# Graph network, node projection: x and its weights split into a high and a low reduced-precision part

## The chip, the cores and the metric

One core of one Trainium2 chip runs the whole program in one launch. The metric is the device time of a launch in microseconds (us), the median of several runs. Beside the timed runs one execution was recorded by the hardware profiler; all rows shown come from it.

## The reference

50,000 nodes with 256 features, 50,000 edges sorted by destination. A graph attention layer, a layer norm, a message-passing layer with a three-layer network, and a second layer norm. The part that matters here is the projection at the start:

```python
loops = jnp.arange(n)                       # a self loop for every node
x_proj = (x @ lin_W.T).reshape(n, 4, 64)    # 50000 x 256 by 256 x 256
s_src = jnp.einsum('nhd,hd->nh', x_proj, att_src)
s_dst = jnp.einsum('nhd,hd->nh', x_proj, att_dst)
att = s_src[src] + s_dst[dst]               # + edge term, leaky relu, softmax over dst
...
out = segment_sum(x_proj[src] * alpha, dst) + bias
x = layernorm(x + out)
x = layernorm(x + message_passing(x, edge_attr_128, src, dst, ...))
```

All arrays are float32.

## The kernel before, in words

The program is a row of blocks with a barrier between them: setup of weights, projection, ranking of the edges by their other end, gathering and attention, the first layer norm with the first products of the second network (`n_` names), the edge network (`u_` names), and the last layer norm. The change touches the setup and the projection block.

**Setup.** The weights are loaded by SyncE and ScalarE queues. VectorE splits the weights of the second network (w0r, w1r, w2r, wgr) into a high part of the type fp32r (a shorter float32 that TensorE takes as one product) and a low part, the rest. TensorE transposes lin_W and multiplies it by the attention vectors; VectorE copies the result from PSUM (the accumulator memory, 8 banks) to `wst`, 128 x 2 x 264: 256 columns of lin_W.T and 8 of attention terms, for two halves of the 256 input features.

**Projection.** The nodes are padded to 98 groups of G = 4 tiles of 128 rows. `groups` writes out four groups, then a loop of two groups a turn, then two more; all engines run the same walk over the groups, and semaphores hold them together. For group g:

- SyncE loads `xin` (128 x 4 x 256), two buffers.
- TensorE (`body`, L382 on) first counts the edges' destination digits: four matmuls of 128 x 392 in f16 from one-hot tiles `ohlo` and `ohhi` into bank 6 (L385), all accumulated over the whole block. It waits for `h_oh`, which VectorE raises once per group, after the fourth pair of one-hot tiles. Then it transposes xin of group g+1 into banks 0 and 1 (`transposes`, L377, eight of 128 x 128). Then come the projections of group g (L394): for each of the four tiles j two float32 matmuls (k = 0, 1) of `xT` with `wst` into bank 2+j, after VectorE has emptied that bank (`pr_d`).
- ScalarE (`both`, L461) copies banks 0 and 1 of group g+1 to `xT`.
- VectorE (`body` from L430) works on two groups at once: for each j it makes the one-hot pair j of group g+1 (`one_hots`, L327 and L328), then waits for the projection of tile j of group g and adds the bias to it (L438, bank to `xps`).
- GpSimd stores `xps` to the DRAM tensor XP.

Each engine takes its instructions in the order in which they are written (TensorE's weight loads may run ahead beside the matmul before them).

Of the kernel before, what the change touches and what calls it, by code (L numbers as in the profile page):

```python
# [21 lines left out]
P = 128  # L22
G = 4
HEADS = 4
# [32 lines left out]
def gnn_kernel(nc, x, src, dst, e128, e32, lin_W, att_src, att_dst, lin_edge_W, att_edge, bias,  # L57
# [90 lines left out]
    with top:  # L148
# [18 lines left out]
        upto = alloc(top, "upto", [P, P])  # L167
        after = alloc(top, "after", [P, P])
        iota = alloc(top, "iota", [P, max(NT, P)], f16)
        wst = alloc(top, "wst", [P, 2, XW])  # L170
        wedge = alloc(top, "wedge", [P, 4 * HEADS])
        biasx = alloc(top, "biasx", [P, XW])

# [14 lines left out]
        with ph:  # L188
# [6 lines left out]
            le4 = alloc(ph, "le4", [P, 2, 4, KE])  # L195
            ab = alloc(ph, "ab", [P, 2, 3 * HEADS])
            ioi = alloc(ph, "ioi", [P, max(NT, P)], i32)
            s_zero, s_load, s_const = sem("w_zero"), sem("w_load"), sem("w_const")
            s_attl, s_mm, s_ev = sem("w_att"), sem("w_mm"), sem("w_ev")
            with nc.Block() as block:  # L200
                @block.gpsimd
# [18 lines left out]
                @block.sync  # L220
                def _(sp):
                    sp.wait_ge(s_zero, 1)
                    with nc.allow_non_contiguous_dma(reason="small weight vectors"):
                        for k, a in enumerate((att_src, att_dst, att_edge)):
                            for h in range(HEADS):
                                r = (h % 2) * HD
                                sp.dma_start(ab[r:r + HD, h // 2, k * HEADS + h:k * HEADS + h + 1],
                                             a[h, :].rearrange("(d a) -> d a", a=1)).then_inc(s_attl, 16)
                        for r, k, a, n in [(0, k, a, n) for k, (a, n) in enumerate(M0[:3])] + \
                                          [(r, 3, A0, R0) for r in STACK]:  # L230
                            sp.dma_start(b0s[r:r + n, k:k + 1], b0[a:a + n].rearrange("(d a) -> d a", a=1))\
                                .then_inc(s_load, 16)
                        for k, (a, n) in enumerate(M1):
                            sp.dma_start(b1s[0:n, k:k + 1], b1[a:a + n].rearrange("(d a) -> d a", a=1))\
                                .then_inc(s_load, 16)
                    sp.wait_ge(s_load, 16 * 9)

                @block.scalar
                def _(act):
                    act.dma_start(lw[:], lin_W.rearrange("(c p) i -> p c i", p=P)).then_inc(s_attl, 16)  # L240
                    for r in range(4):
                        act.dma_start(le4[:, :, r, :], lin_edge_W.rearrange("(c p) k -> p c k", p=P))\
                            .then_inc(s_attl, 16)
                    act.dma_start(biasx[:, 0:D], bias.partition_broadcast(P)).then_inc(s_attl, 16)
                    act.dma_start(w0s[:], W0.rearrange("(c p) m -> p c m", p=P)).then_inc(s_attl, 16)
                    for k, (a, n) in enumerate(M0[:3]):
                        act.dma_start(w1s[0:n, k, :], W1[a:a + n, :]).then_inc(s_attl, 16)
                    act.wait_ge(s_zero, 1)
                    for r in STACK:
                        act.dma_start(w1ts[r:r + R0, :], W1[A0:F0, :]).then_inc(s_attl, 16)  # L250
                    for k, (a, n) in enumerate(M1):
                        act.dma_start(w2s[0:n, k, :], W2[a:a + n, :]).then_inc(s_attl, 16)
                    a, n = M1[-1]
                    act.dma_start(w2s[n:n + 1, 2, :], b2.rearrange("(a d) -> a d", a=1)).then_inc(s_attl, 16)
                    act.dma_start(wgs[:], Wg).then_inc(s_attl, 16)
                    act.wait_ge(s_attl, 16 * (3 * HEADS + 18))

                @block.vector
                def _(dve):
# [4 lines left out]
                    c.did(nc.vector.memset(biasx[:, D:XW], 0.0))  # L264
                    c.did(nc.vector.memset(KI[:, :, NT:NT + G], 0))
                    c.did(nc.vector.memset(wedge[:], 0.0))
                    dve.wait_ge(s_attl, 16 * (3 * HEADS + 18))
                    parts = [(w0r, w0s, P, slice(0, 4)), (wgr, wgs, P, None)]
                    parts += [(w1r, w1s, n, k) for k, (a, n) in enumerate(M0[:3])]
                    parts += [(w2r, w2s, n + (k == 2), k) for k, (a, n) in enumerate(M1)]  # L270
# [11 lines left out]
                            c.did(nc.vector.tensor_copy(w1t[:], w1ts[:]))  # L282
                        c.wait()
                    dve.wait_ge(s_mm, 1)
                    for k in range(2):
                        c.did(nc.vector.tensor_copy(wst[:, k, 0:D], B[k][:, 0:D]))
                    dve.wait_ge(s_mm, 2)
                    for k in range(2):
                        c.did(nc.vector.tensor_copy(wst[:, k, D:XW], B[2 + k][:, 0:8]))
                    c.wait()  # L290
                    for r in range(4):
                        c.did(nc.vector.tensor_copy(wedge[r * KE:(r + 1) * KE, r * HEADS:(r + 1) * HEADS],
# [2 lines left out]
                @block.tensor  # L295
                def _(pe):
                    pe.wait_ge(s_const, 8)
                    pe.wait_ge(s_attl, 16 * (3 * HEADS + 18))
                    for k in range(2):
                        for c in range(2):  # L300
                            t = nc.tensor.transpose(B[k][:, c * P:(c + 1) * P], lw[:, c, k * P:(k + 1) * P], ident[:])
                    t.then_inc(s_mm, 1)
                    for k in range(2):
                        for c in range(2):
                            nc.tensor.matmul(B[2 + k][:, 0:8], lw[:, c, k * P:(k + 1) * P], ab[:, c, 0:8],
                                             start=(c == 0), stop=(c == 1))
                    for c in range(2):
                        t = nc.tensor.matmul(B[4][:, 0:HEADS], le4[:, c, :, :].rearrange("p r k -> p (r k)"),
                                             ab[:, c, 8:12], start=(c == 0), stop=(c == 1))
                    t.then_inc(s_mm, 1)  # L310
# [4 lines left out]
        with srt:  # L315
# [17 lines left out]
            ph = ExitStack()  # L333
            with ph:
                xin = [alloc(ph, f"xin{s}", [P, G, D]) for s in range(2)]
                xT = [alloc(ph, f"xT{s}", [P, 2, G * P]) for s in range(2)]
                xps = [alloc(ph, f"xps{s}", [P, G, XW]) for s in range(2)]
                kr = [alloc(ph, f"key_rows{q}", [P, NC, P], i32) for q in range(2)]
                krf = [alloc(ph, f"key_rowsf{q}", [P, NC, P]) for q in range(2)]
# [2 lines left out]
                tot = [alloc(ph, f"tot{q}", [P, NT]) for q in range(2)]  # L342
                cum = alloc(ph, "cum", [P, NT])
                x_loaded, xp_stored = sems("p_x_loaded"), sems("p_xp_stored")
                xt_psum, xt_a = sem("p_xt_psum"), sem("p_xt_act")
                pr_psum, pr_d = sem("p_pr_psum"), sem("p_pr_dve")
                h_pad, h_loaded, h_rows, h_psum = sem("h_pad"), sem("h_loaded"), sem("h_rows"), sem("h_psum")
                h_chain, h_oh, h_acc, h_hist, h_sums = sem("h_chain"), sem("h_oh"), sem("h_acc"), sem("h_hist"), sem("h_sums")
# [4 lines left out]
                with nc.Block() as block:  # L353
# [17 lines left out]
                    def _(pe):  # L371
                        def transposes(g, s, i, last):
                            pe.wait_ge(x_loaded[s], 16 * (i + 1) + 16 * last)
                            for k in range(2):
                                need(pe, xt_a, 2 * (g - 1) + k + 1)
                                for j in range(G):
                                    t = nc.tensor.transpose(XB[k][:, j * P:(j + 1) * P],  # L377
                                                            xin[s][:, j, k * P:(k + 1) * P], ident[:])
                                t.then_inc(xt_psum, 1)

                        def body(g, s, i, last):
# [5 lines left out]
                            t.then_inc(h_acc, 1)  # L387
                            if not late(g, 1):
                                transposes(g + 1, 1 - s, i if s == 0 else i + 1, late(g, 2))
                            pe.wait_ge(xt_a, 2 * (g + 1))  # L390
                            for j in range(G):
                                need(pe, pr_d, 4 * (g - 1) + j + 1)
                                for k in range(2):
                                    t = nc.tensor.matmul(OB[j][:, 0:XW], xT[s][:, k, j * P:(j + 1) * P], wst[:, k, :],  # L394
                                                         start=(k == 0), stop=(k == 1))
                                t.then_inc(pr_psum, 1)
                        pe.wait_ge(h_rows, 2)
                        for q in range(2):
# [10 lines left out]
                    def _(dve):  # L409
# [13 lines left out]
                        for q in range(2):  # L423
                            c.did(nc.vector.tensor_copy(LO[q][:], ki[q][:]))
                            c.did(nc.vector.tensor_copy(HI[q][:], ki[2 + q][:]))
                        c.wait()
                        for j in range(G):
                            one_hots(0, 0, j, h_oh, (0,))

                        def body(g, s, i, last):  # L430
                            need(dve, xp_stored[s], 16 * i)
                            if not late(g, 1):
                                need(dve, h_acc, g)
                            for j in range(G):
                                if not late(g, 1):
                                    one_hots(g + 1, 1 - s, j, h_oh, (0,))
                                dve.wait_ge(pr_psum, 4 * g + j + 1)
                                nc.vector.tensor_tensor(xps[s][:, j, :], OB[j][:, 0:XW], biasx[:], ALU.add).then_inc(pr_d, 1)  # L438
                        groups(dve, body)
                        dve.wait_ge(h_acc, GROUPS)  # L440
                        nc.vector.tensor_copy(hist[:], HB[:, 0:NT]).then_inc(h_hist, 1)
# [14 lines left out]
                    def _(act):  # L456
                        def both(g, s):
                            need(act, pr_psum, 4 * (g - 1))
                            for k in range(2):
                                act.wait_ge(xt_psum, 2 * g + k + 1)  # L460
                                nc.scalar.copy(xT[s][:, k, :], XB[k][:]).then_inc(xt_a, 1)  # L461

                        def body(g, s, i, last):
                            if not late(g, 1):
# [1319 lines left out]
```

## Time and profile before

| | us |
|---|---|
| median of 3 runs | 5411.32 |
| lowest and highest run | 5406.67, 5420.93 |
| profiled execution | 5421.3 |
| its span | 5419.7 |

| engine | busy us | share of the span |
|---|---|---|
| TensorE matmul (PE) | 4311.3 | 80% |
| TensorE weight load (PEld) | 3429.3 | 63% |
| VectorE (DVE) | 3819.4 | 70% |
| ScalarE (ACT) | 2759.3 | 51% |
| GpSimd (POOL) | 3366.1 | 62% |

The busy shares are means over blocks with different limits. The projection block lies at about 28 to 565 us of the span. In the rows, PEclk and "granted clock" are the mean TensorE clock that the throttle granted, as a share of the full 2.4 GHz; 0.50 is the lower level, 1.2 GHz. A float32 matmul of L394 stands in the trace as two records, every other matmul used here as one. "Idle before" is the time the engine stood still just ahead of an instruction, with what released it. Names are given as out<-in.

### The profile page before, as it was taken

The page shows a single profiled execution, that of the slowest core. Times are in us where ns is not written, and L with a number is a line of the kernel's source. Part 1 is how long each engine was busy: PE and PEld are TensorE (multiplying, and loading weights), DVE is VectorE, ACT ScalarE, POOL GpSimd, SP SyncE. Part 2 cuts the span into 40 slices and gives each one's busy share as a digit, 9 for nine tenths or more (in the row PEclk, how much of TensorE's full clock was granted, in tenths as well). Part 3 has the DMA queues.
Part 4 walks back from the last instruction along what each step waited for, and adds up shares of the span by engine and source line. Part 5 has one row for each costly group of instructions (what it writes and reads, how often), then busy time and mean ns, then how long its engine had stood idle before and what let it go on. Part 6 is the DMA issues. An engine that isn't in the chain of part 4 may idle for free. (4 is left out here: it accounts for less than half of the span.)

```text
span 5419.7 us, 98490 instructions
## 1 busy us (share of the span) xinstructions
PE 4311.3 (80%) x23300; PEld 3429.3 (63%) x23300; DVE 3819.4 (70%) x12680; ACT 2759.3 (51%) x6177; POOL 3366.1 (62%) x3119
## 2 busy tenths in 40 slices
PE   7999777777756676599999997999999999999400
PEld 5777433333334444599999996877877777777300
DVE  5666777777756666798989884766666666666564
ACT  1212233333323333366666665777777777777475
POOL 1111677777777776455555545777777777777432
PEclk9999887888878888799999998999999999999755
DMA  5666100000027666699999995666666666666496
GB/s 159 200 202 200 37 9 9 9 9 9 9 43 195 189 189 188 215 367 353 369 357 369 354 345 148 151 149 150 149 149 150 147 151 147 152 148 150 126 402 278
DMA packets 735369, 966.02 MB, mean 178 GB/s; under 512 B 180881, under 2 KB 634552, under 8 KB 722816
## 3 DMA queue, kind: packets, MB, share of 16 engines
q0 software_dynamic: 183840, 376.00, 30.3%
q10 hardware_dynamic: 216893, 321.19, 16.5%
q1 hardware_dynamic: 334583, 268.27, 15.3%
q8 instruction: 16, 0.26, 0.0%
q14 instruction: 37, 0.30, 0.0%
HBM read 540.38 MB, written 425.15 MB: 178 GB/s over the span
## 5 line engine op out<-in xcount | busy, mean ns | idle before, releaser
L1189 PE MATMUL bank<-w0r,n_x1T 128*128 128x406 f32 x4704 | 905.7, 352 | 34.2 <-ACT n_pa L1237 32.4
L1189 PEld LDWEIGHTS bank<-w0r,n_x1T 128*128 128x128 f32 x4704 | 870.5, 190 | 56.9 <-ACT n_pa L1237 54.4
L1336 POOL DMA_INDIRECT out_x<-u_sums,u_row x392 | 651.9, 1663 | 143.0 <-issue 104.5
L1388 PE MATMUL bank<-u_h,w1r 128*108 128x512 f32 (+1 forms) x2646 | 697.1, 409 | 0.0
L1065 POOL DMA_INDIRECT n_cg<-CT,n_last x392 | 449.5, 1147 | 177.0 <-issue 95.1
L1388 PEld LDWEIGHTS bank<-u_h,w1r 128*108 128x108 f32 (+1 forms) x2646 | 448.1, 176 | 131.8
L681 POOL DMA_INDIRECT xg<-XP,m_src x392 | 436.8, 1114 | 128.6 <-issue 99.1
L576 PE MATMUL bank<-table,ohloT 128*128 128x392 f32 x784 | 433.9, 642 | 84.1 <-DVE rank L621 83.7
L1318 POOL DMA_INDIRECT u_pa<-PA,u_rows x392 | 385.5, 984 | 168.8 <-issue 113.7
L1388 PE MATMUL bank<-w2r,u_h 108*128 108x256 f32 x3528 | 479.6, 280 | 0.0
L520 POOL DMA_INDIRECT DS<-by_dst,rank_int x392 | 388.1, 990 | 121.4 <-issue 107.9
L528 POOL DMA_INDIRECT r_sgather<-XP,r_dst x392 | 381.4, 973 | 126.3 <-issue 119.2
L1318 POOL DMA_INDIRECT u_pb<-PB,u_rows x392 | 385.1, 982 | 119.5 <-issue 119.2
L1388 PEld LDWEIGHTS bank<-w2r,u_h 108*128 108x128 f32 x3528 | 443.6, 188 | 0.1
L328 DVE TENSOR_SCALAR ohhi<-iota,key_hi 128x392 f16<-128x392 f16 x1176 | 401.6, 341 | 0.0
L1376 PE MATMUL bank<-ident,u_pb 128*128 128x128 f32 (+1 forms) x1568 | 243.4, 278 | 158.2 <-DVE u_pb L1552 147.9
L394 PE MATMUL bank<-wst,xT 128*128 128x264 f32 x1568 | 365.8, 387 | 0.0
L477 POOL DMA_DIRECT2D XP<-xps x98 | 74.1, 756 | 462.6 <-DVE xps L438 446.5
L1376 PEld LDWEIGHTS bank<-ident,u_pb 128*128 128x128 f32 (+1 forms) x1568 | 187.0, 138 | 228.6 <-DVE u_pb L1552 161.1
L1552 DVE TENSOR_TENSOR u_pb<-u_pb,u_pa 128x512 f32<-128x512 f32 x294 | 194.5, 689 | 193.9 <-DMA u_pb<-PB,u_rows 193.5
L1481 ACT ACTIVATE u_h<-bank,b1s 108x512 fp32r<-108x512 f32 (+1 forms) x294 | 202.3, 688 | 244.8 <-PE bank L1402 244.8
L461 ACT COPY xT<-bank 128x512 f32<-128x512 f32 x196 | 105.5, 589 | 421.9 <-PE bank L377 421.9
(261 smaller groups left out, 10282.5 us busy)
## 6 DMA issues: line engine op xcount, KB each, us to landing
PA<-n_pa ACTq DMA_DIRECT2D x98, 816.0 KB, 6.1
PB<-n_pb ACTq DMA_DIRECT2D x98, 812.0 KB, 8.9
XP<-xps POOLq DMA_DIRECT2D x98, 528.0 KB, 4.1
CT<-ct ACTq DMA_DIRECT2D x98, 528.0 KB
n_xp<-XP SPq DMA_DIRECT2D x98, 528.0 KB
xin<-in_x SPq DMA_DIRECT2D x97, 512.0 KB, 4.8
n_x<-in_x SPq DMA_DIRECT2D x97, 512.0 KB, 9.8
out_x<-n_x ACTq DMA_DIRECT2D x97, 512.0 KB, 4.9
```

Source lines behind the costliest of these rows:

```text
L328: o = nc.vector.tensor_scalar(ohhi[q][s][:, j, :], iota[:, 0:NT], HI[q][:, t], None, ALU.is_equal)
L394: t = nc.tensor.matmul(OB[j][:, 0:XW], xT[s][:, k, j * P:(j + 1) * P], wst[:, k, :], start=(k == 0), stop=(k == 1))
L520: pool.indirect_dma_start(out=DS, out_offset=bass.IndirectOffsetOnAxis(ap=ri[s][:, j:j + 1], axis=0), in_=pd[s][:, j, :], in_offset=None). ...
L528: pool.indirect_dma_start(out=sg[s][:, j, :], out_offset=None, in_=XP, element_offset=D + HEADS, in_offset=bass.IndirectOffsetOnAxis(ap=ix ...
L576: nc.tensor.matmul(B[ub[b]][:, 0:NT], oT[b][:], tab[b][:], start=True, stop=True)\
L681: pool.indirect_dma_start(out=xg[r][:, j, :], out_offset=None, in_=XP, in_offset=bass.IndirectOffsetOnAxis(ap=sr[r][:, j:j + 1], axis=0))\
L1065: pool.indirect_dma_start(out=cg[s][:, j, :], out_offset=None, in_=CT, in_offset=bass.IndirectOffsetOnAxis(ap=il[s][:, j:j + 1], axis=0)). ...
L1189: o = nc.tensor.matmul(acc, xT[s][p][:, k, e], w0r[q][:, 2 * half + k, :], start=(n == 0), stop=(n == len(terms) - 1))
L1318: pool.indirect_dma_start(out=buf[s][:, j, 0:w], out_offset=None, in_=table, in_offset=bass.IndirectOffsetOnAxis(ap=ix[s][:, 1 - q, j:j + ...
L1336: pool.indirect_dma_start(out=out, out_offset=bass.IndirectOffsetOnAxis(ap=si[s][:, j:j + 1], axis=0), in_=yo[s][:, j, :], in_offset=None, ...
L1376: o = nc.tensor.transpose(TB[k % 2][0:n, j * P:(j + 1) * P], pb[s][:, j, a:a + n], ident[:])
L1388: o = nc.tensor.matmul(acc, a[p], b[q], start=(start and n == 0), stop=(stop and n == 2))
```

## The change

In setup `wst` becomes two fp32r tensors, `wst[0]` the rounded weights and `wst[1]` the rest. In the projection `xT` becomes a high and a low fp32r buffer for each of the two groups in flight. ScalarE's copy writes the high part. A new VectorE step `low` waits for it, subtracts the high part from the bank and writes the low part, and raises a new semaphore `xt_d`; it stands after the bias addition of tiles 0 and 1. TensorE waits for `xt_d` in place of `xt_a`, and each tile's product is six fp32r matmuls (high by high, high by low, low by high, for k = 0 and 1) in place of two float32 ones. In setup one semaphore fewer is used: the loads of the two bias vectors now count on `s_attl`, for which TensorE, VectorE, ScalarE and SyncE all wait.

```diff
--- before.py
+++ after.py
@@ -167,7 +167,7 @@
...
         iota = alloc(top, "iota", [P, max(NT, P)], f16)
-        wst = alloc(top, "wst", [P, 2, XW])
+        wst = [alloc(top, f"wst{q}", [P, 2, XW], f32r) for q in range(2)]
         wedge = alloc(top, "wedge", [P, 4 * HEADS])
@@ -195,7 +195,7 @@
...
             ioi = alloc(ph, "ioi", [P, max(NT, P)], i32)
-            s_zero, s_load, s_const = sem("w_zero"), sem("w_load"), sem("w_const")
+            s_zero, s_const = sem("w_zero"), sem("w_const")
             s_attl, s_mm, s_ev = sem("w_att"), sem("w_mm"), sem("w_ev")
@@ -229,11 +229,11 @@
...
                             sp.dma_start(b0s[r:r + n, k:k + 1], b0[a:a + n].rearrange("(d a) -> d a", a=1))\
-                                .then_inc(s_load, 16)
+                                .then_inc(s_attl, 16)
                         for k, (a, n) in enumerate(M1):
                             sp.dma_start(b1s[0:n, k:k + 1], b1[a:a + n].rearrange("(d a) -> d a", a=1))\
-                                .then_inc(s_load, 16)
-                    sp.wait_ge(s_load, 16 * 9)
+                                .then_inc(s_attl, 16)
+                    sp.wait_ge(s_attl, 16 * (3 * HEADS + 27))
 
...
@@ -282,11 +282,14 @@
...
                     dve.wait_ge(s_mm, 1)
-                    for k in range(2):
-                        c.did(nc.vector.tensor_copy(wst[:, k, 0:D], B[k][:, 0:D]))
                     dve.wait_ge(s_mm, 2)
-                    for k in range(2):
-                        c.did(nc.vector.tensor_copy(wst[:, k, D:XW], B[2 + k][:, 0:8]))
+                    halves = [(k, B[q + k][:, 0:n], slice(a, a + n)) for q, a, n in ((0, 0, D), (2, D, 2 * HEADS))
+                              for k in range(2)]
+                    for k, full, w in halves:
+                        c.did(nc.vector.tensor_copy(wst[0][:, k, w], full))
+                    c.wait()
+                    for k, full, w in halves:
+                        c.did(nc.vector.tensor_tensor(wst[1][:, k, w], full, wst[0][:, k, w].bitcast(f32), ALU.subtract))
                     c.wait()
...
@@ -333,7 +336,7 @@
...
                 xin = [alloc(ph, f"xin{s}", [P, G, D]) for s in range(2)]
-                xT = [alloc(ph, f"xT{s}", [P, 2, G * P]) for s in range(2)]
+                xT = [[alloc(ph, f"xT{s}{q}", [P, 2, G * P], f32r) for q in range(2)] for s in range(2)]
                 xps = [alloc(ph, f"xps{s}", [P, G, XW]) for s in range(2)]
@@ -342,7 +345,7 @@
...
                 x_loaded, xp_stored = sems("p_x_loaded"), sems("p_xp_stored")
-                xt_psum, xt_a = sem("p_xt_psum"), sem("p_xt_act")
+                xt_psum, xt_a, xt_d = sem("p_xt_psum"), sem("p_xt_act"), sem("p_xt_low")
                 pr_psum, pr_d = sem("p_pr_psum"), sem("p_pr_dve")
@@ -372,7 +375,7 @@
...
                             for k in range(2):
-                                need(pe, xt_a, 2 * (g - 1) + k + 1)
+                                need(pe, xt_d, 2 * (g - 1) + k + 1)
                                 for j in range(G):
@@ -387,12 +390,12 @@
...
                                 transposes(g + 1, 1 - s, i if s == 0 else i + 1, late(g, 2))
-                            pe.wait_ge(xt_a, 2 * (g + 1))
+                            pe.wait_ge(xt_d, 2 * (g + 1))
                             for j in range(G):
                                 need(pe, pr_d, 4 * (g - 1) + j + 1)
-                                for k in range(2):
-                                    t = nc.tensor.matmul(OB[j][:, 0:XW], xT[s][:, k, j * P:(j + 1) * P], wst[:, k, :],
-                                                         start=(k == 0), stop=(k == 1))
+                                for n, (k, p, q) in enumerate((k, p, q) for k in range(2) for p, q in ((0, 0), (0, 1), (1, 0))):
+                                    t = nc.tensor.matmul(OB[j][:, 0:XW], xT[s][p][:, k, j * P:(j + 1) * P], wst[q][:, k, :],
+                                                         start=(n == 0), stop=(n == 5))
                                 t.then_inc(pr_psum, 1)
@@ -424,8 +427,15 @@
...
                         c.wait()
+                        def low(g, s, k):
+                            dve.wait_ge(xt_a, 2 * g + k + 1)
+                            nc.vector.tensor_tensor(xT[s][1][:, k, :], XB[k][:], xT[s][0][:, k, :].bitcast(f32),
+                                                    ALU.subtract).then_inc(xt_d, 1)
+
                         for j in range(G):
                             one_hots(0, 0, j, h_oh, (0,))
+                        for k in range(2):
+                            low(0, 0, k)
 
@@ -436,6 +446,8 @@
...
                                 nc.vector.tensor_tensor(xps[s][:, j, :], OB[j][:, 0:XW], biasx[:], ALU.add).then_inc(pr_d, 1)
+                                if j < 2 and not late(g, 1):
+                                    low(g + 1, 1 - s, j)
                         groups(dve, body)
@@ -458,7 +470,7 @@
...
                                 act.wait_ge(xt_psum, 2 * g + k + 1)
-                                nc.scalar.copy(xT[s][:, k, :], XB[k][:]).then_inc(xt_a, 1)
+                                nc.scalar.copy(xT[s][0][:, k, :], XB[k][:]).then_inc(xt_a, 1)
 
```

What stands in a row on VectorE before the change, in a group of the projection that is written out, from its first bias addition (`xps<-bank,biasx`) to the last one-hot tile of the next group (`ohlo` and `ohhi` are a one-hot pair):

```order
L438 TENSOR_TENSOR xps<-bank,biasx 128x264 [waits p_pr_psum]
L327 TENSOR_SCALAR ohlo<-iota,key_lo 128x128
L328 TENSOR_SCALAR ohhi<-iota,key_hi 128x392
L438 TENSOR_TENSOR xps<-bank,biasx 128x264 [waits p_pr_psum]
L327 TENSOR_SCALAR ohlo<-iota,key_lo 128x128
L328 TENSOR_SCALAR ohhi<-iota,key_hi 128x392
L438 TENSOR_TENSOR xps<-bank,biasx 128x264 [waits p_pr_psum]
L327 TENSOR_SCALAR ohlo<-iota,key_lo 128x128
L328 TENSOR_SCALAR ohhi<-iota,key_hi 128x392
```

The same engine and place after the change:

```order
L448 TENSOR_TENSOR xps<-bank,biasx 128x264 [waits p_pr_psum]
L432 TENSOR_TENSOR xT<-bank,xT 128x512 [waits p_xt_act]
L330 TENSOR_SCALAR ohlo<-iota,key_lo 128x128
L331 TENSOR_SCALAR ohhi<-iota,key_hi 128x392
L448 TENSOR_TENSOR xps<-bank,biasx 128x264 [waits p_pr_psum]
L432 TENSOR_TENSOR xT<-bank,xT 128x512 [waits p_xt_act]
L330 TENSOR_SCALAR ohlo<-iota,key_lo 128x128
L331 TENSOR_SCALAR ohhi<-iota,key_hi 128x392
L448 TENSOR_TENSOR xps<-bank,biasx 128x264 [waits p_pr_psum]
L330 TENSOR_SCALAR ohlo<-iota,key_lo 128x128
L331 TENSOR_SCALAR ohhi<-iota,key_hi 128x392
```

Two subtractions (L432) have come between the first bias addition and the last one-hot tile.

TensorE, one group, before, with what each step waits for:

```order
L385 MATMUL bank<-ohhi,ohlo 128x392 [waits h_oh]
L385 MATMUL bank<-ohhi,ohlo 128x392 x3
L377 MATMUL bank<-ident,xin 128x128 [waits p_xt_act,p_x_loaded1]
L377 MATMUL bank<-ident,xin 128x128 x3
L377 MATMUL bank<-ident,xin 128x128 [waits p_xt_act]
L377 MATMUL bank<-ident,xin 128x128 x3
L394 MATMUL bank<-wst,xT 128x264 [waits p_pr_dve,p_xt_act]
L394 MATMUL bank<-wst,xT 128x264
L394 MATMUL bank<-wst,xT 128x264 [waits p_pr_dve]
```

And after:

```order
L388 MATMUL bank<-ohhi,ohlo 128x392 [waits h_oh]
L388 MATMUL bank<-ohhi,ohlo 128x392 x3
L380 MATMUL bank<-ident,xin 128x128 [waits p_xt_low,p_x_loaded1]
L380 MATMUL bank<-ident,xin 128x128 x3
L380 MATMUL bank<-ident,xin 128x128 [waits p_xt_low]
L380 MATMUL bank<-ident,xin 128x128 x3
L397 MATMUL bank<-wst,xT 128x264 [waits p_pr_dve,p_xt_low]
L397 MATMUL bank<-wst,xT 128x264 x5
L397 MATMUL bank<-wst,xT 128x264 [waits p_pr_dve]
```

The steps keep their order; a tile has six matmuls in place of two, and the waits on the copy are now waits on the subtraction.

## Rows read from the trace of the kernel before

**Rows 1.** Stretches: us, each engine's busy us (records), granted clock, DMA share, GB/s.

```profile
core 0: us, PE busy (x) PEld busy (x) DVE busy (x) ACT busy (x) POOL busy (x), PEclk, DMA share, GB/s
300.00:400.00 100.00, 99.45 (x530) 78.92 (x530) 63.05 (x226) 20.41 (x38) 14.30 (x19) 1.00 0.69 201
```

**Rows 2.** Waits, 200 to 400 us: us in total, times, longest.

```profile
DVE xps L438 <- PE bank L394: 60.1, 36, 1.8
PEld bank L385 <- DVE ohhi L328: 16.3, 37, 0.4
```

**Rows 3.** Timeline of one group: start us, us, instruction, count, idle before.

```profile
300.20 0.84 PE L385 MATMUL bank<-ohhi,ohlo 128*128 128x392 f16 x4
...
300.87 1.04 PE L377 MATMUL bank<-ident,xin 128*128 128x128 f32 x8
...
301.51 1.07 ACT L461 COPY xT<-bank 128x512 f32<-128x512 f32 x2 [4.23 <-PE bank L377]
...
301.75 3.73 PE L394 MATMUL bank<-wst,xT 128*128 128x264 f32 x16
...
302.84 0.43 DVE L438 TENSOR_TENSOR xps<-bank,biasx 128x264 f32<-128x264 f32 x1 [1.55 <-PE bank L394]
303.19 0.24 DVE L327 TENSOR_SCALAR ohlo<-iota,key_lo 128x128 f16<-128x128 f16 x1
...
303.73 0.43 DVE L438 TENSOR_TENSOR xps<-bank,biasx 128x264 f32<-128x264 f32 x1
...
305.13 0.32 DVE L328 TENSOR_SCALAR ohhi<-iota,key_hi 128x392 f16<-128x392 f16 x1
305.50 0.45 PEld L385 LDWEIGHTS bank<-ohhi,ohlo 128*128 128x128 f16 x4 [0.44 <-DVE ohhi L328]
```

**Rows 4.** Timeline, VectorE: one-hot tiles of the first group, which wait for nothing.

```profile
42.07 0.32 DVE L328 TENSOR_SCALAR ohhi<-iota,key_hi 128x392 f16<-128x392 f16 x1
42.30 0.25 DVE L327 TENSOR_SCALAR ohlo<-iota,key_lo 128x128 f16<-128x128 f16 x1
42.46 0.32 DVE L328 TENSOR_SCALAR ohhi<-iota,key_hi 128x392 f16<-128x392 f16 x1
```

**Rows 5.** Instruction groups by shape, 2200 to 3180 us: busy us, mean ns, idle before.

```profile
L1140 DVE TENSOR_TENSOR n_x1T<-bank,n_x1T 128x512 fp32r<-128x512 f32 x182 | 116.4, 680 | 0.0
...
L1227 ACT CAST n_x1T<-bank 128x512 fp32r<-128x512 f32 x182 | 98.1, 590 | 126.5 <-PE bank L1189 120.9 <-PE bank L1176 2.9 <-issue 1.5
```

**Rows 6.** Timeline, TensorE: fp32r products of 406 columns in the first layer norm's block.

```profile
2700.78 9.17 PE L1189 MATMUL bank<-w0r,n_x1T 128*128 128x406 f32 x48
2709.79 1.03 PE L1176 MATMUL bank<-ident,n_x 128*128 128x128 f32 x8
```

**Rows 7.** Timeline, TensorE: fp32r products of 256 columns in the edge network.

```profile
4014.53 1.23 PE L1388 MATMUL bank<-w2r,u_h 108*128 108x256 f32 x9
4015.59 0.52 PE L1388 MATMUL bank<-wgr,u_eT 128*128 128x256 f32 x3
```

**Rows 8.** Timeline, VectorE, setup.

```profile
18.87 1.01 DVE L277 CAST w0r<-w0s 128x1624 fp32r<-128x1624 f32 x1 [17.38 <-DMA wgs<-in_L_gnn_Wg]
...
24.98 1.09 DVE L275 TENSOR_TENSOR w2r<-w2s,w2r 108x256 fp32r<-108x256 f32 x3
...
27.29 0.23 DVE L289 COPY wst<-bank 128x8 f32<-128x8 f32 x2
```

**Rows 9.** Stretches of other blocks, and single us of the ranking block.

```profile
600.00:700.00 100.00, 74.74 (x279) 36.71 (x277) 75.86 (x380) 33.03 (x93) 76.42 (x78) 0.86 0.08 9
2200.00:3180.00 980.00, 911.66 (x5032) 884.22 (x5033) 875.43 (x2395) 596.88 (x1354) 539.35 (x560) 0.97 1.02 352
711.00:712.00 1.00, 0.14 (x1) 0.15 (x2) 0.77 (x6) 0.00 (x0) 0.72 (x1) 1.00 0.04 4
...
713.00:714.00 1.00, 0.72 (x2) 0.44 (x3) 1.00 (x8) 0.00 (x0) 0.69 (x2) 0.75 0.04 4
714.00:715.00 1.00, 1.00 (x5) 0.40 (x4) 1.00 (x4) 0.15 (x1) 0.69 (x2) 0.50 0.03 4
```

More of the change, by code:

```diff
@@ L255, in _ @@
                     act.dma_start(wgs[:], Wg).then_inc(s_attl, 16)
-                    act.wait_ge(s_attl, 16 * (3 * HEADS + 18))
+                    act.wait_ge(s_attl, 16 * (3 * HEADS + 27))
                 @block.vector
@@ L266, in _ @@
                     c.did(nc.vector.memset(wedge[:], 0.0))
-                    dve.wait_ge(s_attl, 16 * (3 * HEADS + 18))
+                    dve.wait_ge(s_attl, 16 * (3 * HEADS + 27))
                     parts = [(w0r, w0s, P, slice(0, 4)), (wgr, wgs, P, None)]
@@ L297, in _ @@
                     pe.wait_ge(s_const, 8)
-                    pe.wait_ge(s_attl, 16 * (3 * HEADS + 18))
+                    pe.wait_ge(s_attl, 16 * (3 * HEADS + 27))
                     for k in range(2):
```

## The prediction, made before the changed kernel had run

> **What bounds the kernel now.** The stretches of time come first, since the page's shares average over blocks. In the projection block TensorE is busy 99.45 of 100 us at a granted clock of 1.00, and VectorE only 63.05 [rows 1]. That reads like a block bound by TensorE, into which VectorE's new work would fit. The waits say something else as well: 37 times in 200 us, once a group, TensorE's weight load for L385 waits 0.4 us for VectorE's last one-hot tile, and VectorE waits 1.6 us a group for the first projection [rows 2]. Two engines that wait for each other once a group form a closed chain, so I followed one group in the timeline [rows 3]:
>
> - The projections start at 301.75 and the first bias addition at 302.84: 1.09 us.
> - From there VectorE goes through addition, pair, addition, pair, addition and the first tile of the last pair; its last tile starts at 305.13: 2.29 us.
> - 0.37 us later (305.50) the count of the next group starts on TensorE.
> - The count (300.20 to 300.87, 0.67) and the transposes (to 301.75, 0.88) lead to the next projections: 1.55 us.
>
> The sum is 5.30 us, and the counts at 300.20 and 305.50 lie 5.30 apart. So this chain and TensorE's own work are limits at nearly the same height. Within the 2.29 us VectorE still follows TensorE: additions are 0.89 us apart (302.84, 303.73), a quarter of the projections. Left to itself it would be faster: an addition holds it for 0.35 us (302.84 to 303.19) [rows 3], a tile of ohlo 0.16 and one of ohhi 0.23 where nothing is waited for [rows 4], together 0.74 for addition and pair. The passage would then take 2 x 0.74 + 0.35 + 0.16 = 1.99 us; 0.30 us of it is slack.
>
> **The change part by part.**
>
> *Projections.* Per group 16 float32 records give way to 24 fp32r matmuls of 264 columns. The block shows none of that kind. The nearest rows: 48 of 406 columns take 9.01 us (2700.78 to 2709.79), 188 ns each, 19 ns over their 406 / 2.4 GHz [rows 6]; nine of 256 columns take 1.06 us, 118 ns each, 11 ns over [rows 7]. So 264 columns cost 110 plus 11 to 19 ns, 121 to 129; I take 125. A tile costs 0.75 us in place of 0.89, a group 3.00 in place of about 3.56. TensorE alone would need 1.55 + 3.00 = 4.55 us a group.
>
> The Trainium skill (FP8 and Floating Point Precision, "TensorE Precision Notes") says that true FP32 takes four passes through the array; three single products would be three quarters of them, an estimate of 0.67 us a tile. The rows above say 0.75, because the fixed part of a matmul is paid more often; by the page the loop below would be 0.08 us shorter and the total 8 us less.
>
> *The subtraction.* The same instruction exists later: 128x512, bank and SBUF to fp32r, 680 ns [rows 5]. An addition of 0.43 us releases VectorE after 0.35, so I charge 0.60 a piece, 1.20 a group, with 0.68 as the upper bound. It stands twice between the first addition and the last one-hot tile. It never waits: the two copies it needs run from 301.51 for 1.07 us and end at 302.58, before the first addition has started [rows 3]; writing fp32r costs ScalarE nothing, 590 ns against half of 1.07 us [rows 3, 5]. Queued behind it on VectorE are the pairs 1 to 3 of the next group, on which `h_oh` hangs, and on `h_oh` the count, the transposes and all later projections. In the likeliest case nothing covers it but the 0.30 us of slack.
>
> *The chain after.* Projections to first addition: 1.09 - 0.89 + 0.75 = 0.95. VectorE: 1.99 + 1.20 = 3.19. To the count: 0.37. Count and transposes: 1.55. Together 6.06 us, 0.76 more than 5.30, and above TensorE's 4.55. The last addition no longer lies in the chain: it runs beside the count. There are 98 groups, so 97 such steps: +74 us. Bounds: without the slack (2.29 + 1.36 in place of 3.19) and with the dear matmul it is 6.54, +120 us; with 121 ns a matmul 6.04, +72.
>
> *Waits moved from the copy to the subtraction.* The transposes of a group need both subtractions of the group before. These end about 2 us after its first addition at the latest, the transposes start over 1.5 us later. Nothing.
>
> *Setup.* VectorE is the last engine there. It gets four subtractions: 0.36 us apiece for the two of 256 columns (three take 1.09), 0.12 for the two small ones (two copies take 0.23), and a wait between: +1.0 us [rows 8]. The nine small loads of the bias vectors are now waited for; VectorE starts at 18.87 when the last weight has landed [rows 8]. They could land later by 0 to 1 us; I take 0. The subtractions of group 0 run beside the first count: 0.
>
> *End of the block.* The last group makes no pairs and no subtractions; its projections are shorter by 0.6 us: -0.6.
>
> Sum: 74 + 1.0 - 0.6 = +74 us on the profiled execution's 5421.3, that is 5496. That execution lies 10 us above the median of the runs, 5411.3, so against the median I forecast 5411.3 + 74 = 5485.
>
> **The rivals.**
>
> *A: the clock falls too.* TensorE would work 4.55 of 6.06 us, 75%. In the ranking block it is busy 74.7% of 100 us and its granted clock is 0.86; the single microseconds show it: after one with 0.14 busy the clock sinks in the third (0.75) and is 0.50 in the next [rows 9]. Against it: in that block TensorE starves for several microseconds, here every pause of 1.5 us is followed by 4.5 us without a break, and at 93% busy the clock is 0.97 [rows 9]. Price, at the ranking block's 0.86: 0.28 of the time at half speed, where TensorE binds with 2 x 4.55 = 9.1 us a group. The mean is 1 / (0.72 / 6.06 + 0.28 / 9.1) = 6.69 us, 1.39 over now: +135, so 5411 + 135 = 5546.
>
> The Trainium skill (TensorE: Matmul & The Clock Gate, "A second HAM failure mode: psum-queue depth-cycling") describes just this rival: frequent short pauses between groups of matmuls make the clock swing between its two levels. The fall in rows 9 agrees that waits bring it down; no row shows pauses as short and regular as the new ones.
>
> *B: VectorE's work is hidden, the kernel is faster.* VectorE is 63% busy [rows 1], and 1.20 us more in a group is 86%. If the count did not wait for the last pair, or VectorE could make the pairs while it waits, TensorE would set the pace: 4.55 plus the 0.2 us by which the chain shows today, 4.75, -0.55 a group, -53 us: 5358. It decides where VectorE's passage is shorter than the three tiles after the first (2.25 us), less 0.2 for the hand-over. It is 3.19 by rows 3 to 5, and VectorE's idle 1.6 us lies where the next pairs may not start in its order. It needs an error of a third in measured durations.
>
> *C: the split is not cheaper on TensorE.* If a fp32r matmul cost what a float32 record costs (0.22 us), a tile would take 1.33 us and a group 5.3 + 1.55 = 6.9 us on TensorE: +1.6 x 97 = +155, 5566. Rows 6 and 7 speak against it.
>
> *D: no change.* The chain would have to hide 1.0 of the 1.20 us. Only a much longer slack than the 0.30 us would give it.
>
> **How the numbers follow.** Forecast 0.73, A 0.16 (in part or in full), B 0.05, C 0.03, D 0.03. Predicted 5485. The forecast's own range is 5470 to 5535: the bounds +72 and +120, with the runs' spread of about 10 us. At the top it takes in the milder half of A. I give 5465 to 5540. A difference of 0.3% (16 us) is what a measurement of this kernel can tell from none. Faster by more: 0.05 (B); within: 0.03 (D); slower: 0.92.
>
> **What would show it.** In the profile after: counts 6.0 to 6.1 us apart; TensorE and VectorE both near 75% busy in the block; TensorE's wait for the last one-hot tile up from 0.4 to some 1.8 us a group; additions 1 and 2 starting without a wait; the wait of VectorE for its first addition about as now; 24 matmuls in 3.0 us; subtractions of 0.68 us; the block's end near 640 us, and all later blocks as long as before. The forecast is wrong if the granted clock in the block is under 1.00 (A), if the counts come 4.8 us apart (B), or if 24 matmuls need over 5 us (C).

## The result and the profile after

| | before, us | after, us |
|---|---|---|
| median of 5 runs | 5411.39 | 5487.77 |
| lowest, highest | 5406.67, 5420.93 | 5473.53, 5495.96 |
| span of the profiled execution | 5419.7 | 5480.8 |

The ratio is 1.0134, 95% interval 1.0117 to 1.0151. The change makes the kernel 76 us slower; 5485 was forecast. On another chip the same kernel measured 5490.9 against 5418.2, ratio 1.0137 (1.0122 to 1.0153).

One group in the timeline of the kernel after (start us, us, engine, instruction, idle before), the counterpart of [rows 3]:

```profile
300.29 0.45 PEld L388 LDWEIGHTS bank<-ohhi,ohlo 128*128 128x128 f16 x4 [1.60 <-DVE ohhi L331]
300.30 0.84 PE L388 MATMUL bank<-ohhi,ohlo 128*128 128x392 f16 x4 [1.39 <-DVE ohhi L331]
...
300.97 1.04 PE L380 MATMUL bank<-ident,xin 128*128 128x128 f32 x8
...
301.76 3.17 PE L397 MATMUL bank<-wst,xT 128*128 128x264 f32 x24
...
302.78 0.43 DVE L448 TENSOR_TENSOR xps<-bank,biasx 128x264 f32<-128x264 f32 x1 [1.80 <-PE bank L397]
303.13 0.68 DVE L432 TENSOR_TENSOR xT<-bank,xT 128x512 fp32r<-128x512 f32 x1
303.73 0.24 DVE L330 TENSOR_SCALAR ohlo<-iota,key_lo 128x128 f16<-128x128 f16 x1
...
304.12 0.42 DVE L448 TENSOR_TENSOR xps<-bank,biasx 128x264 f32<-128x264 f32 x1
304.46 0.68 DVE L432 TENSOR_TENSOR xT<-bank,xT 128x512 fp32r<-128x512 f32 x1
...
305.95 0.32 DVE L331 TENSOR_SCALAR ohhi<-iota,key_hi 128x392 f16<-128x392 f16 x1
...
306.32 0.84 PE L388 MATMUL bank<-ohhi,ohlo 128*128 128x392 f16 x4 [1.39 <-DVE ohhi L331]
```

The projections end at 304.93 (301.76 + 3.17) in place of 305.48 [rows 3], so TensorE is done sooner. But the last one-hot tile starts at 305.95 and the next count at 306.32. VectorE works from 302.78 to that tile without a gap; only its first addition waits. The counts lie 6.02 us apart.

The waits of the kernel after, 200 to 400 us (in total, times, longest), and the stretch from 300 to 400 us (busy us and records of each engine, granted clock, DMA share, GB/s):

```profile
DVE xps L448 <- PE bank L397: 59.8, 34, 1.8
PEld bank L388 <- DVE ohhi L331: 52.9, 33, 1.6
```

```profile
300.00:400.00 100.00, 77.38 (x604) 70.16 (x605) 69.42 (x231) 18.28 (x34) 12.79 (x17) 1.00 0.58 175
```

Against [rows 2] the weight load's wait for the last pair has grown from 0.4 to 1.6 us a group. Against [rows 1] TensorE has fallen from 99.45 to 77.38 us busy, at an unchanged clock of 1.00.

Setup in the kernel after (VectorE's first instruction and the split of wst), against [rows 8]:

```profile
19.82 1.01 DVE L277 CAST w0r<-w0s 128x1624 fp32r<-128x1624 f32 x1 [18.33 <-DMA b1s<-in_L_gnn_b]
...
27.57 0.90 DVE L289 CAST wst<-bank 128x256 fp32r<-128x256 f32 x4
28.51 0.90 DVE L292 TENSOR_TENSOR wst<-bank,wst 128x256 fp32r<-128x256 f32 x4
```

VectorE starts 0.95 us later, now released by a small bias load, and the four subtractions take another 0.9 us: +1.9 us.

Where the 61 us of the two profiled executions lie is read from one instruction group of the ranking block and one of the last block (duration, first and last start). Before:

```profile
L528 POOL DMA_INDIRECT r_sgather<-XP,r_dst x392: 940/967/1190, 573.4 to 1572.2; - x196
...
L1752 ACT ACTIVATE f_y<-f_y,f_shift,f_rstd x392: 583/585/601, 5130.3 to 5400.8; 128x256 f32<-128x256 f32 x196
```

After:

```profile
L540 POOL DMA_INDIRECT r_sgather<-XP,r_dst x392: 940/963/1188, 643.7 to 1641.1; - x196
...
L1764 ACT ACTIVATE f_y<-f_y,f_shift,f_rstd x392: 583/585/601, 5194.2 to 5461.9; 128x256 f32<-128x256 f32 x196
```

The ranking block starts 70.3 us later and the end comes 61.1 us later: the whole loss arises by the end of the projection, and the blocks behind it ran 9 us shorter in this execution, about the spread of the runs. (The execution profiled before lies 10 us above its median and the one after 5 us below, which is why 61 stands here and 76 between the medians.)

### The profile page after: what moved, and what is told of

Same layout as the page of the kernel before. It is cut to its first block and busy times, and to the rows that moved or that the text cites. A ratio compares the mean times of both kernels' runs of the same rounds, so it can differ in the third digit from the quotient of the medians.

```text
span 5480.8 us, 100442 instructions
## 1 busy us (share of the span) xinstructions
PE 4246.9 (77%) x24084; PEld 3435.7 (63%) x24084; DVE 3906.6 (71%) x12880; ACT 2759.6 (50%) x6177; POOL 3360.9 (61%) x3119
## 5 line engine op out<-in xcount | busy, mean ns | idle before, releaser
L473 ACT CAST xT<-bank 128x512 fp32r<-128x512 f32 x196 | 105.6, 590 | 490.4 <-PE bank L380 490.4
L796 PE MATMUL bank<-msg,m_sel 128*128 128x260 f32 x784 | 264.3, 495 | 76.0 <-DVE msg L743 72.1
```

Of the source, the lines that this page charges most:

```text
L796: nc.tensor.matmul(SB[j][:, 0:MW], sel[s][:, j, :], msg[s][:, j, :], start=True, stop=True)\
```

## The experiments

For each kernel the group's time below is the distance from the first to the last record of the count in the block, over 97 (before: 43.6 to 560.5 us, 5.33; after: 45.4 to 631.8, 6.05, which takes in the first, slower group). Its difference from 5.33, times 97, should be the change in time if nothing else moves.

| kernel | us a group | x 97 | measured, us | ratio (95%) |
|---|---|---|---|---|
| after | 6.05 | +70 | +76 | 1.0134 (1.0117 to 1.0151) |
| VectorE's half alone | 6.21 | +86 | +91 | 1.0166 (1.0152 to 1.0180) |
| TensorE's half alone | 4.87 | -44 | -44 | 0.9914 (0.9898 to 0.9929) |
| one subtraction behind the last pair | 5.46 | +13 | +16 | 1.0028 (1.0019 to 1.0037) |
| both behind it | 5.25 | -7 | -7 | 0.9987 (0.9978 to 0.9996) |
| both behind it, store's wait later | 5.04 | -28 | -31 | 0.9954 (0.9932 to 0.9976) |
| one behind it, store's wait later | 5.48 | +15 | +15 | 1.0033 (1.0021 to 1.0045) |
| pairs first, split kept | 4.77 | -54 | -57 | 0.9901 (0.9886 to 0.9916) |
| pairs first, float32 products | 5.12 | -20 | -30 | 0.9950 (0.9930 to 0.9969) |
| four subtractions | 7.58 | +218 | +206 | 1.0314 (1.0272 to 1.0356) |

The sixth, ninth and tenth row of the table, and a first measurement of the eighth (-59 us, ratio 0.9900, 0.9869 to 0.9930), come from a chip on which the kernel before took 6305 us. It was not profiled there. In the four kernels that were, blocks behind the projection are longer: the ranking block takes 1421 to 1433 us in place of 999 (first to last gather), the edge network 2101 to 2120 in place of 1760 (first to last `u_h`). The projection block is not: with the pairs first its group takes 4.77 us on both chips. So the us compare there, the ratios less so.

**The two halves apart.** VectorE's half alone keeps the subtractions and the waits on them; `xT[s][0]` and `wst[0]` are float32 in it:

```diff
-    for n, (k, p, q) in enumerate((k, p, q) for k in range(2) for p, q in ((0, 0), (0, 1), (1, 0))):
-        t = nc.tensor.matmul(OB[j][:, 0:XW], xT[s][p][:, k, ...], wst[q][:, k, :], ...)
+    for k in range(2):
+        t = nc.tensor.matmul(OB[j][:, 0:XW], xT[s][0][:, k, ...], wst[0][:, k, :], ...)   # float32
```

> Only VectorE's half of the change: the subtractions and the waits on them stand as in the changed kernel, but the projections are the two float32 matmuls a tile on a float32 copy; the low parts are written and not used. Theory: 1.09 to the first addition, 3.17 on VectorE, 0.37, 1.47: 6.10 us a group, +0.80 x 97 = +78 and +2 in setup: 5491 us, as slow as the full change or 0 to 10 us more. Rival (the fp32r matmuls cost the time): near 5411. Rival (VectorE's waits are slack): 5411 to 5430.

TensorE's half alone takes the subtractions out, and TensorE waits for the copy again:

```diff
-    low(0, 0, k)
-    if j < 2 and not late(g, 1):
-        low(g + 1, 1 - s, j)
-    ... matmul(OB[j][:, 0:XW], xT[s][p][:, k, ...], wst[q][:, k, :], ...)
+    ... matmul(OB[j][:, 0:XW], xT[s][0][:, k, ...], wst[q][:, k, :], ...)
```

> Only TensorE's half of the change: six fp32r matmuls a tile, all on the high part of x, no subtraction of x (its low part is left out of the result), waits on the copy as before. Theory: 1.02 + 1.97 + 0.37 + 1.47 = 4.83 us a group, -46 + 2 = -44 us: 5367 us, equal to the kernel with the subtractions behind the last pair within 10 us. Rival (the cheaper matmuls give nothing, or pauses bring the clock down): 5411 or more, granted clock in the block under 1.00.

By this edit the third product of each k is high by high once more, so the result counts that part twice. The number and the shapes of the matmuls are those of the change, and only their time is asked for.

Measured: 5512.5 and 5378.1 us against 5421.8 of the kernel before on that chip. The first came 11 us above its forecast on that base (5502, 80 more than before): its group is 6.21, not 6.10. The second came where the theory put it. The halves in their timelines, first VectorE's alone, then TensorE's alone:

```profile
300.79 0.84 PE L388 MATMUL bank<-ohhi,ohlo 128*128 128x392 f16 x4 [0.91 <-DVE ohhi L331]
...
302.34 3.73 PE L397 MATMUL bank<-wst,xT 128*128 128x264 f32 x16
...
303.43 0.43 DVE L448 TENSOR_TENSOR xps<-bank,biasx 128x264 f32<-128x264 f32 x1 [1.97 <-PE bank L397]
```

```profile
300.58 3.15 PE L397 MATMUL bank<-wst,xT 128*128 128x264 f32 x24
...
303.94 0.84 PE L388 MATMUL bank<-ohhi,ohlo 128*128 128x392 f16 x4 [0.20 <-DVE ohhi L331]
```

With float32 products the way from the count to the projections is 1.55 us, and to the first addition 1.09; I had put 1.47 for the first, the fp32r kernel's. With it the sum is 6.18. So the gain and the loss of the change are both there, and they don't add: -44 and +91 make +47, the whole is +76. While VectorE's chain sets the pace, the cheaper projections save only what lies in the chain: 0.07 us a group up to the first addition and 0.08 between the count and the projections.

**Where the subtraction stands.** Behind the last pair, ahead of the last addition:

```diff
     one_hots(g + 1, 1 - s, j, h_oh, (0,))
+    if j == G - 1:
+        for k in range(2):
+            low(g + 1, 1 - s, k)
     dve.wait_ge(pr_psum, 4 * g + j + 1)
     ...
-    if j < 2 and not late(g, 1):
-        low(g + 1, 1 - s, j)
```

> Both subtractions stand behind the last one-hot pair and ahead of the last addition, all else as in the changed kernel. Theory (the chain over the last pair sets the group's time): it loses the 1.20 us of subtraction, 1.02 + 1.97 + 0.37 + 1.47 = 4.83 us a group, perhaps 0.1 more where the second half of the transposes waits for the second subtraction; against 5.30 before that is -46 to -36 us over 97 groups, +2 in setup: 5367 to 5377 us. TensorE waits for the last pair about 0.4 us a group. Rival (VectorE's load as such sets the time, wherever the subtraction stands): no change from 5488. Rival (six fp32r matmuls are the cost): 5488.

And one on each side (`low(g + 1, 1 - s, 0)` after addition 0, `low(g + 1, 1 - s, 1)` where the two stand above):

> One subtraction after the first addition as in the changed kernel, the other behind the last one-hot pair. Theory: each subtraction ahead of the last pair costs its full 0.60 us: 4.83 + 0.60 = 5.43 us a group, +0.13 x 97 = +13 and +2: 5426 us, halfway between the two ends. Rival (a threshold: VectorE's slack takes the first one and the second makes the loss): near 5370 us. Rival (load as such): 5488.

Measured against 5421.8: 5414.4 and 5437.5 us. The one on each side came as the chain has it (+16, forecast +15). From none ahead of the last pair to one to two, the group goes from 4.87 (TensorE's half alone) to 5.46 to 6.05 us: 0.59 us for each, with no threshold. Both behind the pair should have come within 10 us of TensorE's half alone. They came 36 us above it and brought only 7 of the 34 to 44 us. The subtractions are out of the chain there, but TensorE still waits for the last pair, 0.65 us a group: something else makes it late. Its waits, 200 to 400 us:

```profile
DVE ohlo L330 <- DMA XP<-xps: 34.9, 38, 1.3
PEld bank L388 <- DVE ohhi L331: 25.4, 39, 0.9
PEld bank L380 <- DVE xT L432: 12.1, 78, 0.2
```

VectorE stands 0.9 us a group ahead of its first one-hot tile, because the body begins with the wait that the buffer `xps` has been stored. The DMA issues of the same stretch (count, KB, median us to landing), first of this kernel, then of the kernel before:

```profile
XP<-xps POOLq DMA_DIRECT2D x38, 528.0 KB, 5.2
xin<-in_x SPq DMA_DIRECT2D x38, 512.0 KB, 3.8
```

```profile
XP<-xps POOLq DMA_DIRECT2D x38, 528.0 KB, 4.1
xin<-in_x SPq DMA_DIRECT2D x38, 512.0 KB, 4.9
```

The store lands after 5.2 in place of 4.1 us, the load after 3.8 in place of 4.9. The last addition comes later, so the store is issued just behind the load (301.21 after 301.01) and no longer ahead of it (301.39 before 302.09). The order of the two issues is not the whole of it. With one subtraction on each side the store is issued 0.27 us ahead of the load (303.89 and 304.16), and both land late:

```profile
XP<-xps POOLq DMA_DIRECT2D x37, 528.0 KB, 5.5
xin<-in_x SPq DMA_DIRECT2D x37, 512.0 KB, 5.4
```

**The store's wait.** It guards only what the first addition writes, so it may stand there:

```diff
-    need(dve, xp_stored[s], 16 * i)
     ...
     for j in range(G):
         ...
+        if j == 0:
+            need(dve, xp_stored[s], 16 * i)
         dve.wait_ge(pr_psum, 4 * g + j + 1)
```

> As the kernel with both subtractions behind the last pair, but VectorE waits for the store of xps just ahead of the first addition, which writes that buffer, and not ahead of the first one-hot pair. Theory (what took the gain there was VectorE's wait for a store that lands after 5.2 us in place of 4.0): the wait of 0.9 us a group goes, the chain is 4.83 us plus 0.1 at the transposes, -0.37 x 97 + 2 = -34 us against before: ratio 0.9937. Rival (the collision of load and store slows both, so the wait only moves on to the addition): ratio 0.997 to 0.999, as it was.

> One subtraction ahead of the last pair and one behind it, with the wait for the store moved to just ahead of the first addition. Theory: the store is then no longer waited for, and the chain with one subtraction in it is 1.02 + 2.57 + 0.37 + 1.47 = 5.43 us a group: +0.13 x 97 + 2 = +15 us against before, ratio 1.0027. Rival (the store's later landing still binds, at the addition): as with the wait at its old place, over 5.5 us a group and 1.004 or more; there it measured 1.0028 in time, so the group's time decides more than the ratio.

Measured: -31 us (6274.0 against 6305.1) and +15 us (5433.3 against 5418.2). The landing is still 5.2 us in the first, but VectorE waits for it once in 200 us, not 38 times, and the group falls from 5.25 to 5.04; the sum had 4.93. Its timeline shows 1.61 us from count to projections (304.44 to 306.05) in place of 1.47, since the transposes wait twice for a subtraction; with that the sum is 4.97. So the store's wait took 20 us (by the groups) to 24 us (by the times) of the missing gain, and the transposes' waits some 14 (0.14 x 97). With one subtraction on each side the wait cost nothing: the group's time is 5.46 with it at its old place and 5.48 at the new, in spite of a landing of 5.5 us. There VectorE has the time to spare.

**Pairs first.** Pairs 0 and 1, addition 0, pairs 2 and 3, addition 1, subtraction, addition 2, subtraction, addition 3, with the store's wait at the first addition:

```diff
+    if j < 2:
+        pairs((2 * j, 2 * j + 1))            # one_hots of group g+1
     dve.wait_ge(pr_psum, 4 * g + j + 1)
     ...
-    if j < 2 and not late(g, 1):
-        low(g + 1, 1 - s, j)
+    if j in (1, 2) and not late(g, 1):
+        low(g + 1, 1 - s, j - 1)
```

> The changed kernel with VectorE's order turned round: pairs 0 and 1, addition 0, pairs 2 and 3, addition 1, subtraction, addition 2, subtraction, addition 3, and the store's wait ahead of the first addition. Theory: the last pair is ready before TensorE's projections end, so TensorE sets the pace: 1.47 + 3.0 = 4.5 us, with 0.1 to 0.2 where the second half of the transposes waits for a subtraction: 4.6 to 4.75 us a group, -0.55 to -0.68 x 97 + 2: ratio 0.988 to 0.991, the fastest. Rival (VectorE's load of 4.4 us a group and the store's landing of 5.2 us bind before that): 4.9 us or more, ratio 0.993 or more.

> The same kernel as the one with the pairs first, beside the changed kernel on one chip. Theory: 4.76 us a group as measured there, -0.54 x 97 + 2 = -51 us against before. If the blocks behind the projection run as in the kernel before: ratio 0.9906 at 5410 us. Rival (the gain belongs to that chip, whose ranking block ran 1.4 times as long): a ratio of 0.996 or more here.

The same order of pairs in the kernel before, with its float32 products:

> The kernel before the change (float32 products) with pairs 0 and 1 ahead of addition 0 and pairs 2 and 3 ahead of addition 1. Theory (chain and TensorE's work lie close together before the change): the chain is taken away, TensorE alone needs 1.5 + 3.5 = 5.1 us a group in place of 5.30: -0.2 x 97 = -20 us, ratio 0.9963. Rival (before, TensorE alone sets the time): ratio 1.000.

Measured: 5361.5 us against 5418.2 and 5490.9 of the changed kernel on the same chip, the lowest ratio of all (the interval of TensorE's half alone overlaps with it). The forecast was 4.6 to 4.75 us a group; it is 4.77. With float32 products -30 us (6275.1 against 6305.1), of which the block shows 20. The stretch from 300 to 400 us, the split with pairs first, then float32 with pairs first:

```profile
300.00:400.00 100.00, 98.44 (x761) 87.72 (x759) 89.35 (x296) 24.65 (x42) 15.81 (x21) 1.00 0.68 226
```

```profile
300.00:400.00 100.00, 100.00 (x553) 83.57 (x551) 64.47 (x236) 21.48 (x40) 15.08 (x20) 1.00 0.71 208
```

In both TensorE no longer waits for the last pair and works almost without a break. With the split it is still held a little: in 200 us its weight loads for the transposes wait 44 times, 12.9 us in all, for a subtraction, and VectorE's first addition 31 times, 17.1 us in all, for the store. So the second limit is near. The split is worth 5.12 - 4.77 = 0.35 us a group, 34 us, once VectorE's order lets it through (29 us between the times of the two kernels on that chip); the order is worth 20 us by itself. The two kernels differ in the place of the store's wait as well; with float32 products VectorE waits for the store 5 times in 200 us, so that matters little.

**Does the clock follow?** Each subtraction made twice, the second result going nowhere:

> The changed kernel with every subtraction made twice (the second result goes to a tile that nobody reads): four of them stand between the first addition and the last pair. Theory (each costs its full 0.60 us, clock at its upper level): 6.02 + 1.20 = 7.22 us a group, +116 us over the changed kernel, ratio to before about 1.035. Rival A of the prediction (longer pauses, TensorE 62% busy, bring the clock down): granted clock in the block under 1.00 and ratio 1.045 or more.

Measured +206 us over before. The theory says +192 (116 and the 76 of the change), rival A at least +243 (0.045 of 5411). A group without a fall of the clock is 7.22 us by the theory; of the 97 distances from count to count 68 are 7.2 us, and the other 29 are 8.0 to 9.6. The mean is 7.58. The stretch from 400 to 500 us:

```profile
400.00:500.00 100.00, 66.90 (x489) 60.98 (x490) 71.74 (x214) 15.35 (x28) 10.54 (x14) 0.95 0.47 143
```

One of the longer groups and the start of the next, on TensorE:

```profile
370.37 0.84 PE L389 MATMUL bank<-ohhi,ohlo 128*128 128x392 f16 x4 [2.60 <-DVE ohhi L331]
371.04 1.54 PE L381 MATMUL bank<-ident,xin 128*128 128x128 f32 x8
372.24 4.33 PE L398 MATMUL bank<-wst,xT 128*128 128x264 f32 x24
378.68 0.84 PE L389 MATMUL bank<-ohhi,ohlo 128*128 128x392 f16 x4 [2.11 <-DVE ohhi L331]
```

It takes 8.31 us at a granted clock of 0.79, its projections 4.33 in place of 3.15; the groups on both sides take 7.2 us at 1.00. TensorE pauses 2.6 us in most groups, and the granted clock is 0.93 over the block (0.91 from 200 to 300 us, 0.97 from 300 to 400). So rival A exists, at twice the subtractions: 0.36 x 97 = 35 us of the 218 us in the block. At the change's 1.4 us it does not: 1.00 from 100 us to the end of the block, and 96 of the 97 distances are 6.0 us.

## Why the prediction was right

By its own steps:

- *The chain.* Forecast and measured: projections to first addition 0.95 and 1.02; VectorE 3.19 and 3.17; to the count 0.37 and 0.37; count and transposes 1.55 and 1.47; together 6.06 and 6.02. Two errors of 0.07 and 0.08 cancel, which is luck. Since TensorE's half alone is faster, VectorE's half alone slower than the whole, and a subtraction costs its full time (0.59 us) only where it stands ahead of the last pair, the chain is shown and not only argued.
- *The total.* 76 us against a forecast of 74 is closer than the parts: the loop gained 70 us (+74 forecast), setup 2, and the end of the block gave back 1. That makes the 70.3 us by which the ranking block starts later. The other 6 us between the medians lie within the spread of the runs. For the profiled execution 5496 was forecast, and it took 5482.
- *The subtraction.* 0.60 us of VectorE each (303.13 to 303.73), as charged; it never waited. The fp32r copy on ScalarE costs nothing more, as said, though half of 1.07 us was the wrong number to set beside its 590 ns: two copies overlap in that row, and one of them takes 589 ns in the kernel before.
- *The projections.* 24 matmuls in 3.17 us with the last one's tail; 125 ns apart ((3.17 - 0.287) / 23, with the mean record of 287 ns). By three quarters of a float32 tile, the estimate that the prediction worked out from the Trainium skill (FP8 and Floating Point Precision, "TensorE Precision Notes"), it would have been 111 (0.75 x 0.89 / 6). The measurement decides for the rows.
- *Waits on the subtraction at the transposes:* none in the changed kernel, as said.
- *Setup.* +1.0 forecast, +1.9 measured; the 0.95 us by which the bias loads land later were inside the bound and left out of the sum.
- *The other blocks* should stay as they were. They did within 9 us in the profiled execution.
- *Rival A* did not occur, but appears when the pause is doubled. The Trainium skill (TensorE: Matmul & The Clock Gate, "A second HAM failure mode: psum-queue depth-cycling") describes such a swing for frequent short pauses between groups of matmuls; the runs here agree for pauses of 2.6 us (granted clock 0.93 over the block), not for pauses of 1.4 us (1.00). *Rival B* fails on the order, as argued: with pairs first and the same work on VectorE the kernel is faster by 57 us, close to the 53 that B was priced at. The price is met in part by luck: the 0.2 us that it adds to TensorE's own work stood for the last pair, and what the runs show in that place are the transposes' waits for a subtraction. *Rival C*: TensorE's half alone is 44 us faster, so it falls.

What I did not see was the second limit behind the first, the store's landing, which took most of the gain when the subtractions were moved. Nothing measured here says why the landing times change so with the spacing of the two issues, why the blocks behind the projection take up to 10 us more or less from run to run, nor why the ranking block and the edge network were slow on one chip.

## What to carry to other kernels

When two engines wait for each other once per step, work added to the less busy one costs its time, less the slack that lies there, if it stands between the two waits. Elsewhere it costs less, until the next limit is met (here the store's landing and the transposes' wait). Follow one round of the chain before trusting a busy share. An order that raises the hand-over first is worth trying before the arithmetic is changed. A wait should stand directly ahead of the instruction that it guards: that was worth 20 to 24 us where the engine had no time to spare, and nothing where it had.

## What the runs showed of the hardware

- How soon two half-megabyte transfers land depends on how they are spaced. Store and load take 4.1 and 4.9 us with the store issued 0.7 us ahead, 5.5 and 5.4 with it 0.27 us ahead, 5.2 and 3.8 with the load 0.2 us ahead.
- TensorE's clock stayed at its upper level with a pause of 1.4 us in every 6.0 us, and fell at times with 2.6 us in every 7.2: 29 of 97 groups took 8.0 to 9.6 us, and the granted clock was 0.93 over the block.
- A float32 product of 264 columns costs two records 0.22 us apart, three fp32r ones 0.125 each: 0.375 in place of 0.44 us.
